# A decoder's second attention: two steps a tick for the last group's middle stage, and no pause ahead of batch 4

## What is computed

```
x = LN(x + attn0(x))         16 heads of 64
x = LN(x + xattn0(x, ctx))   one head of 128, softmax, biases
x = LN(x + ffn0(x))          one matrix, scaled by the best gate probability
x = LN(x + attn1(x))         16 heads of 8, causal, biases
x = LN(x + xattn1(x, ctx))   rotated q and k, decay mask, no softmax
x = LN(x + ffn1(x))          512 wide, silu gate, ternary weights, 8 bit activations
```

## The kernel before

| step | PE | ACT | DVE | POOL |
|---|---|---|---|---|
| 0 | context products L629, L506 | copies L916, L918 | moments L1135, L1138 | rsqrt L431-L434 |
| 2 | | normalise L906 | | |
| 3 | transpose x L617 | copy L911 | | |
| 4 | query product L637 | copy L925 | | |
| 5 | scores L506 | | L1152, L1153 | |
| 6 | | exponential L928 | | |
| 7 | transpose L644 | copy L931 | L1156, L1157 | |
| 8 | output L506 | | L1163 | |
| 9 | | | moments | rsqrt |
| 11, 12 | transpose x L617 | normalise, copy | | |
| 13 | FFN L656 | | L1174-L1177 | |
| 14, 15 | | exponential L938 | L1180-L1184, moments | rsqrt |
| 17, 18 | transpose x L617 | normalise, copy | | |
| 19-21 | products L663, L665, L506 | L948, L951 | L1190, L1194, L1199 | |

## Time and profile before

### The profile page before, as it was taken

One profiled execution on the slowest core, in us unless ns is written; L12 is line 12 of the kernel. 1 busy time (PEld: TensorE's weight loads), 2 busy tenths in 40 slices (PEclk: granted clock), 3 DMA queues, 4 the chain that ended last, 5 costly groups with the idle time before them and its releaser, 6 DMA issues.

```text
span 329.0 us, 6840 instructions
## 1 busy us (share of the span) xinstructions
PE 250.3 (76%) x2655; PEld 190.5 (58%) x2658; DVE 216.4 (66%) x538; ACT 148.2 (45%) x274; POOL 67.0 (20%) x102
## 2 busy tenths in 40 slices
PE   0858688988999989799967899999886667652430
PEld 0836567878787878687845566666564434240110
DVE  3996995679657996865356656567476756354662
ACT  5864662275437736144422354543525552202651
POOL 8900000000011001171114681352020002021002
PEclk9989999999999999999978999999999995655555
DMA  7985541344133502436000620004000000000011
GB/s 235 388 224 165 121 102 66 115 96 114 66 106 88 130 3 85 130 103 100 2 1 0 134 26 2 0 18 90 0 3 2 1 2 0 0 0 1 0 32 32
DMA packets 27679, 22.86 MB, mean 69 GB/s; under 512 B 19136, under 2 KB 24256, under 8 KB 26944
## 3 DMA queue, kind: packets, MB, share of 16 engines
q1 hardware_dynamic: 27648, 22.43, 25.9%
HBM read 12.20 MB, written 6.03 MB: 55 GB/s over the span
## 4 chain that ended last, share of the span: by engine, by line
PE 48%; DVE 28%; ACT 11%; issue 7%; POOL 3%; DMA 1%; ACTq 0%; DVEq 0%; POOLq 0%
DVE arena L1076 7%; PE PS L506 4%; ACT arena L883 3%; PE PS L683 3%; PE PS L579 3%; PE PS L606 3%; ACT xt L906 3%; PE PS L705 2%; DVE rowmax L1081 2%; PE PS L598 2%; PE PS L547 2%; POOL rstd L433 2%; PE PS L689 2%; PE PS L532 2%; PE PS L688 2%
## 5 line engine op out<-in xcount | busy, mean ns | idle before, releaser
L431 POOL TENSOR_SCALAR shift<-mv 128x3 f32<-128x3 f32 (+2 forms) x15 | 3.6, 240 | 243.2 <-DVE mv L1138 243.2
L1076 DVE TENSOR_TENSOR arena<-PS,arena 64x512 f16<-64x512 f32 x64 | 44.1, 690 | 6.7 <-ACT arena L883 5.1
L883 ACT ACTIVATE arena<-PS 64x512 f16<-64x512 f32 x64 | 37.8, 591 | 19.2 <-PE PS L534 18.4
L532 PE MATMUL PS<-xh,w0l 128*128 128x256 f32 x64 | 21.7, 339 | 17.0 <-DVE w0l L1067 9.5
L962 ACT ACTIVATE PT<-PS 128x512 f32<-128x512 f32 x32 | 19.1, 595 | 34.2 <-PE PS L689 34.1
L906 ACT ACTIVATE xt<-res,shift,rstd 128x128 f32<-128x128 f32 x42 | 17.7, 483 | 32.6 <-POOL shift L434 32.5
L1211 DVE TENSOR_REDUCE rowmax<-PS 128x4 f32<-128x512 f32 x32 | 21.9, 688 | 13.5 <-PE PS L691 13.1
L896 ACT ACTIVATE PT<-PS 128x512 f32<-128x512 f32 x32 | 19.1, 597 | 16.0 <-PE PS L563 14.5
L532 PEld LDWEIGHTS PS<-xh,w0l 128*128 128x128 f32 x64 | 13.4, 209 | 19.4 <-DVE arena L1076 9.7
L579 PE MATMUL PS<-V,PT 128*64 128x68 f32 x512 | 22.2, 229 | 1.9 <-DVE On L1105 1.9
L561 PE MATMUL PS<-arena 128*128 128x128 f16 x128 | 23.3, 221 | 0.3 <-DVE MR L1088 0.3
(11 more groups left out here) (206 smaller groups left out, 652.1 us busy)
## 6 DMA issues: line engine op xcount, KB each, us to landing
arena<-arena SPq DMA_DIRECT2D x8, 512.0 KB, 5.1
v_piece<-VN SPq DMA_DIRECT2D x8, 512.0 KB, 2.7
V<-v_piece SPq DMA_DIRECT2D x64, 64.0 KB, 2.5
arena<-k_piece SPq DMA_DIRECT2D x4, 192.0 KB, 4.4
arena<-q_piece SPq DMA_DIRECT2D x4, 192.0 KB, 6.3
q_piece<-VN SPq DMA_DIRECT2D x6, 96.0 KB, 1.7
xT<-x_T SPq DMA_DIRECT2D x1, 512.0 KB, 3.8
w<-wk SPq DMA_DIRECT2D x2, 256.0 KB, 4.6
```

What stands on the lines that cost most here:

```text
L532: mm(dst, w0l[:, w, g], xh[:, x], start=True, stop=False)
L883: m = fn(dst[:, a], src[a * 64:(a + 1) * 64], ACT.Copy)
L1076: m = tt(lower[:, a], src[a * 64:(a + 1) * 64], upper[:, a], ALU.subtract)
```

## The change

Two numbers of the schedule change. `GAP` is 0 in place of 2, so that batches 4 to 7 start two ticks earlier. Group 2's middle stage gets the places (0, 2) of each tick in place of place 1.

```diff
-GAP = 2
+GAP = 0
...
-        at = plan("mid", 2, *max((at[0] + 1, 0), (4 * LAST[2] + 7, 0)), (1,))
+        at = plan("mid", 2, *max((at[0] + 1, 0), (4 * LAST[2] + 7, 0)), (0, 2))
```

## The result

The change makes the kernel slower: 343.45 us (median of 4 runs, 339.87 to 344.33) against 332.69 us (332.2 to 333.38). The ratio is 1.032, with a 95% interval of 1.027 to 1.037. That is 10.8 us more, where 8.4 us were forecast; the profiled execution took 344.33 us, its span is 342.5 us, 13.5 us more than before. It is the slowest of the four executions, so terms read from it may lie above what the median shows.

A forecast was written before the change was run, and what follows sets the result against it. The prediction took the stretch before group 3 as bound by PE and the tail by latency. Its terms, 7.7 - 1.2 - 2.35 + 4.25 = +8.4 us, added to the median 333.19, gave 341.6 us, range 336.0 to 346.5.

The forecast's parts named there:

- waits between paired steps: Group 2's middle stage: PE stalls where a step needs ACT's or DVE's result of the step before; plus 7.7 us.
- a fall of the clock in the stretch: Sign of being wrong: PE's clock falling between batch 0's K scores and group 3's start.
- What bounds the stretch: Second attention, 185.4 to 225.0 us: bound by PE, busy 37.88 of 39.6 us, ticks shrinking with PE's work.
- Rival A: Attention ticks have a floor of their own and stalls vanish in them; 3.9 us faster, 329.3 us; chance 0.08.
- Term 1: Group 2's two steps a tick: six stalls of PE, plus 7.7 us, bounds 4.3 and 9.3.
- step 18's: Group 2: PE waits for step 18's trip of about 5.75 us, with 4.2 us of work between; stall 1.55 us.
- Term 2: No pause before batches 4 to 7: nothing in sum, minus 1.2 us where attention meets group 3, between 0 and minus 3.
- The credit of 1.2 us: At 249.28 us, PE's 1.23 us wait for copy L974 behind group 3's normalisation goes, as the copy changes tick.
- Term 3 and 4: Group 3's FFN step 16 leaves the attention, minus 2.35 us; the rest lengthens the tail, plus 4.25 us.
- The part that was worked out from rows: Tail, between L1143 and L1292: a batch's finish and group 3's moments lie bare in the chain; plus 3.65 us.
- Rival C: PE's clock falls in a stall, 2.5 us lost each: 344.1 us with one fall, 346.6 with two; chance 0.2.

The follow-up runs named there:

- e5_spread: The change, with group 2's steps spread over ticks u = 5 to 20 so dependent steps have a whole tick between; 333.8 us, ratio to before 1.004.
- the pairs alone: The kernel before, with only group 2's middle stage at places (0, 2) and GAP still 2; 345.0 us.
- e6_norm: e5_spread, with group 3's second normalisation half a tick later, behind the attention's copy; 330.3 us, ratio to before 0.992.
- the kernel with room at the roots: The change, with group 2 also skipping a whole tick behind each of steps 0, 9 and 15; 337.3 us.
- e1_gap: The kernel before, with only GAP = 0 and group 2 still at one step a tick; 343.3 us.
- e8_warm: The change, with seven unread matmuls ahead of each of group 2's first two groups of transposes, inside PE's long waits; 342.5 us.
- e10_warm: e8_warm run once more, beside a repeat of the change; 341.2 us, ratio to before 1.030.
- e7_ffn: e6_norm, with group 3's FFN steps two ticks earlier; 331.7 us.
- a9_change: The change itself, unaltered, run once more; 345.6 us, ratio to before 1.040.

## Why the prediction was right

The time lies in the range, on the side forecast, 1.9 us above the number given. The main mechanism, waits between paired steps, is what happened. But the nearness of the number is in part luck. In the profiled executions the forecast was +8.4 us and the change is +13.5; group 3's start was forecast at 235.5 us and came at 241.4. One of the prediction's own signs of being wrong, a fall of the clock in the stretch, came true. By its own steps:

**What bounds the stretch.** Right. PE's ticks had no room for a second step's trip: in 56.1 us it was busy 46.6 (83%, forecast some 84%). Rival A, the ticks with room in them, is refuted: PEld's share went down from 67% to 57%, and the stretch became 15 us longer.

**Term 1, the six waits.** Forecast 1.9, 0.65, 0.65, 2.2, 1.55 and 0.75, 7.7 us in all; measured 1.89, 0.56, 0.64, 2.33, 1.11 and 0.47, 7.0 us. The one off most is step 18's: its trip (from L1174 at 209.16 to PE's transpose at 214.65) was 5.5 us for the 5.75 forecast, and PE's two ticks were a little longer. (The upper bound of this term, six times a quarter us more, is 9.2 us and not 9.3; nothing rests on it.) With room between the steps nearly all of it went again (e5_spread, where one wait of 0.56 us is left), which shows the cause.

**Term 2, the pause.** Its main part agrees with the runs: worth nothing in sum, as the pairs alone are as slow as both edits, within a spread of 4 to 7 us. The credit of 1.2 us was wrong. PE's wait of 1.23 us for L974 did go, but the step that ended it there, group 3's normalisation, now stands ahead of another copy, L969, and L722 waits 1.92 us for that. The step that failed: I looked at what leaves the queue behind L906 and not at what comes into its place. e6_norm shows the cause.

**Term 3 and 4, the FFN step and the tail.** From group 3's start to the last batch's end, 6.5 us less were forecast (225.0 to 271.5 against 235.5 to 275.5); measured 5.7 us less, with a fall of the clock in it. In the tail 4.25 us more were forecast and 2.9 us measured, at a mean clock of 0.61 where before had 0.56. The part that was worked out from rows fits: from L1143 to L1292 it is 312.44 - 307.85 = 4.59 us, and before 298.86 - 297.90 = 0.96, so 3.63 us more where 3.65 were forecast; the finish of the batch and the moments fill it. What the whole tail loses goes with the clock. At about the same clock as before (0.55) the kernel with room at the roots, with the tail order of the change, takes 31.3 us, 3.9 more than before. At 0.68 the same order takes 28.4 to 29.2 us (e1_gap, e5_spread, e6_norm, e8_warm, e10_warm), 1.0 to 1.8 more than before, and about 2 more than the order of before at 0.63 (26.6 us in e7_ffn).

**Rival C, the clock.** It had a chance of 0.2, and it came on top of the forecast. In the profiled execution both waits, 1.89 and 2.33 us, were followed by a fall; in a9_change only the longer one. The price in this stretch is 56.05 - 53.1 = 2.95 us for two falls and 54.35 - 53.1 = 1.25 us for one, about 1.5 us each where 2.5 was taken from the 5 us at half clock of the earlier trace rows; these falls were shorter (0.50 from 190.8 to 194.2 us and from 204.5 to 207.9). Two falls at the price taken would have been 346.6 us. The step that failed in the number given is thus that it priced the clock at nothing. With the waits filled the kernel takes 342.5 and 341.2 us in its two sets, near the 341.6 forecast; but it still has the wait of 1.92 us that was not foreseen, with a fall behind it, and a shorter tail loss than forecast, so misses of both signs meet there.

**What stays open.** Of the 15.2 us of the table's second line 3.1 are work moved ahead, 7.0 the six waits, 2.95 the clock, and 1.06 two more waits of L722 (0.53 each), 14.1 in all; the last us has no place of its own. And whether a fall comes is not decided by the wait's length alone: the 1.89 us wait brought one in one execution of the change and none in another (a9_change) nor in the pairs alone, where one of 1.09 us did.

## What to carry to other kernels

On an engine that works through its queue in order and is nearly full, a step costs its own time only if its operands are ready when its turn comes. Before putting two dependent steps next to each other, add up the trip through the other engines and subtract what stands between them in the queue; that gave six waits here to within half a microsecond. Then ask the same of every step that moves into the place of one that left, and allow for a stall on TensorE costing more than its length: here a fall of the clock behind it cost about 1.5 us, and did not come every time.

## What was not expected

The spread of a kernel's runs goes with the clock. In the ten runs of e5_spread the time goes from 330.0 us at a mean granted clock of 0.903 to 336.1 us at 0.873, in step with it; the kernel before has the same (330.2 us at 0.907, 335.3 us at 0.881, of 25 runs). One profile can be 4.6 us off the median of its kernel (e1_gap: 338.7 profiled, 343.3 median).
